# Turning three instead of two of sixteen key blocks on the vector engine in a graph-attention stage

## The reference, cut to what matters

```python
q = (x @ Wq + bq).reshape(n, H, C)      # H, C = 4, 32
attn = jnp.einsum('nhc,mhc->hnm', q, k) / np.float32(np.sqrt(C))
mask = adj == 0.0
neg = jnp.where(mask[None], -jnp.inf, attn)
e = jnp.where(mask[None], 0.0, jnp.exp(neg - jnp.where(all_inf, 0.0, m)))
alpha = e / jnp.where(denom == 0.0, 1.0, denom)
out = jnp.einsum('hnm,mhc->hnc', alpha, v)
```

## Time and profile before

| | |
|---|---|
| median of 3 runs | 1786.12 us (1785.13 to 1786.65) |
| the profiled execution | 1782.96 us, its span 1781.3 us |
| PE busy | 1735.9 us (97%) |
| DVE busy | 1228.6 us (69%) |
| ACT busy | 975.8 us (55%) |
| POOL busy | 895.6 us (50%) |
| mean of DMA | 218 GB/s |

### The profile page before, as it was taken

The page is one execution under the profiler, slowest core; times in us unless marked ns, Lnnn a source line. Parts: engine busy times, 40 slices in busy tenths (PEclk is TensorE's granted clock), DMA queues, the critical chain, the costliest instruction groups (busy, mean ns, idle before and its releaser), DMA issues.

```text
span 1781.3 us, 40266 instructions
## 1 busy us (share of the span) xinstructions
PE 1735.9 (97%) x15000; PEld 1131.3 (64%) x15000; DVE 1228.6 (69%) x2405; ACT 975.8 (55%) x1505; POOL 895.6 (50%) x849
## 2 busy tenths in 40 slices
PE   7999999999998999999999999999999999999996
PEld 3444444444444778877877887778778777644442
DVE  4777775222225889999999999999999999301322
ACT  0110111010103898999999999999999999411101
POOL 0212120112114755778878788788787896540211
PEclk9999999999998999999999999999999999999998
DMA  9866676899996544445445445454454543897981
GB/s 382 325 221 251 254 252 224 278 313 371 332 366 184 186 155 161 155 155 167 150 140 182 150 152 170 156 173 150 142 178 144 167 157 116 323 371 275 321 323 57
DMA packets 134029, 388.53 MB, mean 218 GB/s; under 512 B 15712, under 2 KB 66144, under 8 KB 109280
## 3 DMA queue, kind: packets, MB, share of 16 engines
q1 hardware_dynamic: 117792, 356.11, 57.6%
q10 hardware_dynamic: 13824, 22.75, 3.6%
q0 software_dynamic: 2240, 7.34, 1.6%
HBM read 333.19 MB, written 52.95 MB: 217 GB/s over the span
## 4 chain that ended last, share of the span: by engine, by line
PE 92%; DVE 4%; issue 1%; ACT 1%; DMA 1%; POOL 1%; DVEq 0%; ACTq 0%; POOLq 0%; SPq 0%
PE bank L592 35%; PE bank L742 23%; PE bank L763 14%; PE bank L701 13%; DVE arena L1281 2%; PE bank L580 1%; PE bank L655 1%; PE bank L614 1%; PE bank L613 1%; DMA arena<-x_dram 1%; PE bank L607 0%; PE bank L769 0%; PE bank L650 0%; PE bank L789 0%; PE bank L630 0%
## 5 line engine op out<-in xcount | busy, mean ns | idle before, releaser
L976 ACT ACTIVATE arena<-arena,small 128x2048 f32<-128x2048 f32 x256 | 516.2, 2016 | 2.8 <-DVE small L1281 2.8
L742 PE MATMUL bank<-ident,arena 128*128 128x128 f32 x3592 | 485.5, 278 | 4.4 <-ACT arena L976 2.6
L742 PEld LDWEIGHTS bank<-ident,arena 128*128 128x128 f32 x3592 | 398.1, 141 | 87.8 <-issue 41.9
L592 PE MATMUL bank<-arena,stat_s 128*128 128x512 f32 x1008 | 439.1, 592 | 2.1 <-issue 1.2
L988 ACT ACTIVATE arena<-bank 128x512 f32<-128x512 f32 x673 | 377.0, 604 | 66.2 <-PE bank L742 65.3
L701 PE MATMUL bank<-k,parts 128*128 128x512 f32 x1024 | 354.4, 436 | 10.6 <-DVE small L1281 10.6
L592 PEld LDWEIGHTS bank<-arena,stat_s 128*128 128x128 f32 x1008 | 189.2, 190 | 226.8 <-issue 225.4
L763 PE MATMUL bank<-arena,stat_x 128*32 128x128 f32 x8192 | 276.5, 276 | 0.0
L763 PEld LDWEIGHTS bank<-arena,stat_x 128*32 128x32 f32 x8192 | 208.1, 109 | 90.8 <-issue 81.5
L592 PE MATMUL bank<-arena,stat_x 128*128 128x512 f32 x512 | 228.3, 598 | 10.1 <-DMA arena<-adj_cols 7.8
L701 PEld LDWEIGHTS bank<-k,parts 128*128 128x128 f32 x1024 | 158.8, 192 | 29.6 <-DVE small L1281 24.5
(11 more groups left out here) (155 smaller groups left out, 1431.8 us busy)
## 6 DMA issues: line engine op xcount, KB each, us to landing
arena<-adj_cols SPq DMA_DIRECT2D x190, 1024.0 KB, 6.4
stat_s<-adj SPq DMA_DIRECT2D x85, 512.0 KB, 4.8
group_dram<-stat_s SPq DMA_DIRECT2D x63, 512.0 KB, 2.9
arena<-group_dram SPq DMA_DIRECT2D x252, 128.0 KB, 2.8
arena<-adj SPq DMA_DIRECT2D x43, 512.0 KB, 4.6
parts<-q_dram SPq DMA_DIRECT2D x128, 64.0 KB, 2.4
k<-k_dram POOLq DMA_DIRECT2D x28, 256.0 KB, 9.5
x_dram<-arena ACTq DMA_DIRECT2D x16, 256.0 KB, 3.7
```

What stands on the lines that cost most here:

```text
L592: mm_ = pe.matmul(bank[:, to, :], stat[:, jt, :], ring[:, s, j, :], start=(jt == 0), stop=(jt == TILES - 1))
L742: last = pe.transpose(bank[:, b_, h * P:(h + 1) * P], cols[:, st % SETS, h, u * P:(u + 1) * P], ident[:, :])
L976: act.activation(cols[:, s_, h, :], cols[:, s_, h, :], ACT.Exp, bias=shift[:, t % 2, 1, i:i + 1], scale=-1.0, accum_out=blocksum[:, t % 2, ...
```

## The change: what it does

Units 13, 14 and 15 are turned in blocks, at places 1, 2 and 6, as one group of three. PE turns 13 units a set, 104 a chunk (before 112); in the last set all 16, as before. `slot_of` and `used_before` number the turned slots by PE's units alone. The group gets slots of its own in `stat_s` and `blocks` moves to chunks 5 to 7 of it. One of three mask buffers goes, masks are loaded 7 ahead, and chunks 0 to 5 of `xt` are spilled. The attends run in three batches, at 4, 8 and 14. SP's order becomes: group's store, mask, group's loads, mask, xt's store, queries. The tables of copies and exponents are new: DVE copies 23 of 104 units a chunk (before 28 of 112), ACT 81 (before 84). DVE's `hh` goes from place 113 to 115, ACT's logarithms from 119 to 121. The last product waits for all of `xt` before its first slot, not before its third; `load_xt` also waits for the last group's attends.

```diff
-ATTEND_BATCH = 4
-ATTEND_LAG = 8
-BLOCK_TURN_AT = {14: 3, 15: 5}
-GROUPS = ((14, 15),)
-VECTOR_PLACES = (6,)
-VECTOR_ALSO = (3, 9, 17, 21, 23, 25, 37, 49, 53, 58, 61, 64, 81, 82, 84, 89, 90, 103, 109, 114, 119, 121, 125)
-VECTOR_NOT = (22, 54, 118)
-EXP_MOVED = {1: 3, 5: 7, 13: 12, 21: 22, 29: 28, 37: 39, 45: 44, 49: 51, 53: 54, 57: 58, 61: 60, 69: 70, 73: 74, 77: 76, 81: 83, 85: 84, 89: 87, 93: 90, 101: 103, 105: 106, 109: 108, 113: 114, 121: 122, 125: 124}
+ATTENDS = {4: (-4, -3, -2, -1), 8: (0, 1, 2, 3, 4, 5), 14: (6, 7, 8, 9, 10, 11)}
+BLOCK_TURN_AT = {13: 1, 14: 2, 15: 6}
+GROUPS = ((13, 14, 15),)
+VECTOR_PLACES = ()
+VECTOR_ALSO = (5, 6, 7, 19, 25, 27, 38, 54, 58, 59, 66, 69, 82, 86, 87, 91, 92, 97, 99, 103, 119, 121, 123)
+VECTOR_NOT = ()
+EXP_MOVED = {9: 6, 13: 12, 17: 18, 21: 22, 25: 26, 29: 27, 33: 34, 37: 38, 41: 40, 45: 44, 49: 52, 53: 55, 57: 58, 61: 60, 65: 67, 69: 70, 73: 72, 77: 76, 81: 82, 89: 86, 93: 91, 97: 99, 101: 102, 105: 103, 109: 108, 117: 119, 125: 123}
...
-MASK_AHEAD = 8
-MASKS = 3
-SPILLED = (2, 3, 4, 5)
+MASK_AHEAD = 7
+MASKS = 2
+SPILLED = (0, 1, 2, 3, 4, 5)
...
+def slot_of(k):
+
+    return (PE_UNITS + LAST_UNITS).index(k) % TURNED
+
+
+def used_before(c, k):
+
+    i = (PE_UNITS + LAST_UNITS).index(k) - TURNED
+    return c * UPC + PE_UNITS[i] + 1 if i >= 0 else (c - 1) * UPC + PE_UNITS[i] + 1
...
-        group_slots = arena[:, RING + 10 * CHUNK:RING + 12 * CHUNK]
-        adj_in = (arena[:, RING + 4 * CHUNK:RING + 6 * CHUNK], spilled[:, 0:2 * CHUNK], spilled[:, 2 * CHUNK:4 * CHUNK])
+        adj_in = (arena[:, RING + 4 * CHUNK:RING + 6 * CHUNK], spilled[:, 0:2 * CHUNK])
+        group_slots = spilled[:, 2 * CHUNK:5 * CHUNK]
+        blocks = [stat_s[:, TILES - 3 * TPC:TILES, :].rearrange("p t f -> p (t f)")]
...
-                if g * UPS + GROUPS[i][-1] >= TURNED:
-                    sp.wait_ge(unit_used, g * UPS + GROUPS[i][-1] - TURNED + 1)
+                if g > 0:
+                    sp.wait_ge(unit_used, (g - 1) * UPS + GROUPS[i][-1] + 1)
...
-                    load_mask_ahead(c, 2 * st + 0)
                     if g < GROUP_SETS:
                         store_group(g, 0)
+                    load_mask_ahead(c, 2 * st - 1 if g == 0 else 2 * st)
+                    if g < GROUP_SETS:
+                        load_group(g, 0)
+                    if g == 0:
+                        load_mask_ahead(c, 2 * st)
+                    load_mask_ahead(c, 2 * st + 1)
                     if st == 0 and c - 2 in SPILLED:
                         store_xt(c - 2)
-                    if g < GROUP_SETS:
-                        load_group(g, 0)
                     if st % SETS == 0:
...
-                    load_mask_ahead(c, 2 * st + 1)
...
+                sp.wait_ge(unit_used, GROUP_SETS * UPS)
...
-                    if (k - ATTEND_LAG) % ATTEND_BATCH == 0:
-                        for a in range(k - ATTEND_LAG, k - ATTEND_LAG + ATTEND_BATCH):
-                            if a >= 0:
-                                attend(c, a, first)
-                            elif not first:
-                                attend(c - 1, UPC + a, False)
+                    for a in attended_at(c, k):
+                        if a >= 0:
+                            attend(c, a, first)
+                        elif not first:
+                            attend(c - 1, UPC + a, False)
...
-            product(2, 0, {0: [final_out], SPILLED[0] - 1: [lambda: pe.wait_ge(xt_in_place, 16 * len(SPILLED))], 5: [lambda: pe.wait_ge(att_pool, AG(last - 1, "xt"))],
+            pe.wait_ge(xt_in_place, 16 * len(SPILLED))
+            product(2, 0, {0: [final_out], 5: [lambda: pe.wait_ge(att_pool, AG(last - 1, "xt"))],
```

More of the change, by code:

```diff
@@ L122 @@
 LAST_UNITS = [k for k in range(UPC - UPS, UPC) if k % UPS in BLOCK_TURN_AT]
+LAST_BY_VECTOR, LAST_BY_SCALAR = LAST_UNITS[0::2], LAST_UNITS[1::2]
 def is_block_turned(c, k):
@@ L198, in last_bank_before, with attended_at @@
     return TURN_BANKS.uses[LAST_USE + 1 + LAST_UNITS.index(k) - len(TURN_BANKS.BANKS)][1]
+def attended_at(c, k):
+    u = k % UPS
+    return [k - u + a for a in ATTENDS.get(u, ())]
+def slot_of(k):
[3 more added lines that the diff above has]
+    return c * UPC + PE_UNITS[i] + 1 if i >= 0 else (c - 1) * UPC + PE_UNITS[i] + 1
 BY_VECTOR = [k for k in PE_UNITS if (k % 16 in VECTOR_PLACES or k in VECTOR_ALSO) and k not in VECTOR_NOT]
@@ L287, in build_program @@
         cols = arena[:, 0:RING].rearrange("p (s h n) -> p s h n", s=2, h=H)
+        spilled = stat_s[:, SPILLED[0] * TPC:(SPILLED[-1] + 1) * TPC, :].rearrange("p t f -> p (t f)")
         turned = [stages[i] for i in (0, 1, 6, 7, 2, 3, 10, 11)]
-        group_slots = arena[:, RING + 10 * CHUNK:RING + 12 * CHUNK]
-        spilled = stat_s[:, SPILLED[0] * TPC:(SPILLED[-1] + 1) * TPC, :].rearrange("p t f -> p (t f)")
-        adj_in = (arena[:, RING + 4 * CHUNK:RING + 6 * CHUNK], spilled[:, 0:2 * CHUNK], spilled[:, 2 * CHUNK:4 * CHUNK])
-        tail = stat_s[:, TILES - 2 * TPC:TILES, :].rearrange("p t f -> p (t f)")
-        blocks = [tail if len(group) == 2 else spilled[:, 2 * CHUNK:3 * CHUNK] for group in GROUPS]
+        adj_in = (arena[:, RING + 4 * CHUNK:RING + 6 * CHUNK], spilled[:, 0:2 * CHUNK])
+        group_slots = spilled[:, 2 * CHUNK:5 * CHUNK]
+        blocks = [stat_s[:, TILES - 3 * TPC:TILES, :].rearrange("p t f -> p (t f)")]
         maskbias = [half_[:, i * BLOCK:(i + 1) * BLOCK] for half_ in
@@ L305, in slots_of @@
         def slots_of(i):
-            first, n = GROUPS[i][0] % TURNED - 6, len(GROUPS[i])
-            return group_slots[:, first * CHUNK:(first + n) * CHUNK]
+            return group_slots[:, 0:len(GROUPS[i]) * CHUNK]
         def tiles(ap):
@@ L541, in _ @@
                              q_parts[:, i, :].bitcast(F32)).then_inc(gcn_q_out, 16)
-            load_mask(0, 5)
+            load_mask(0, 4)
             sp.wait_ge(gcn_dve, CV(last, "root"))
             sp.dma_start(root_dram[:, last * CHUNK:CHUNKS * CHUNK], root_out).then_inc(gcn_root_out, 16)
-            for m in range(6, MASK_AHEAD):
+            for m in range(5, MASK_AHEAD - 1):
                 load_mask(0, m)
@@ L761, in attend @@
                     else:
-                        weights = turned[k % TURNED][:, h * P:(h + 1) * P]
+                        weights = turned[slot_of(k)][:, h * P:(h + 1) * P]
                     last = pe.matmul(to, stat_x[:, k % UPT, h * C:(h + 1) * C], weights,
@@ L815, in attention @@
                 if last_chunk:
-                    for a in range(UPC - ATTEND_LAG, UPC):
+                    for a in range(UPC - 4, UPC):
                         attend(c, a, first)
@@ L981, in copy_unit @@
                 if not (first and k < TURNED):
[L982 to L988 removed]
+                    act.wait_ge(unit_used, used_before(c, k))
+                elif k >= TURNED - 2:
+                    act.wait_ge(gcn_x2_out, 16 * CHUNKS)
+                elif k >= TURNED - 4:
+                    act.wait_ge(gcn_k_out, 32 * CHUNKS)
+                act.activation(turned[slot_of(k)], bank[:, unit_bank(k), :],
                                ACT.Copy).then_inc(unit_copied_act, 1)
@@ L1049, in attention @@
                         block_weights(c, k // UPT)
-                    if k in BY_SCALAR or (last_chunk and k == LAST_UNITS[1]):
+                    if k in BY_SCALAR or (last_chunk and k in LAST_BY_SCALAR):
                         copy_unit(c, k, first)
@@ L1377, in attention @@
             def attention(c, first, last_chunk):
-                post = post_steps(c - 1, 107 if last_chunk else 113) if not first else {}
+                post = post_steps(c - 1, 107 if last_chunk else 115) if not first else {}
                 for k in range(UPC):
@@ L1397, in attention @@
                             turn_blocks(c, k - place + u)
-                    if k in BY_VECTOR or (last_chunk and k == LAST_UNITS[0]):
+                    if k in BY_VECTOR or (last_chunk and k in LAST_BY_VECTOR):
                         copy_unit(c, k, first)
```

38 lines of the change are left out of this document (14 added, 24 removed).

## The result

| | before | after |
|---|---|---|
| median of 4 runs | 1785.83 us (1785.13 to 1786.65) | 1815.13 us (1809.0 to 1816.66) |
| the profiled execution | 1782.96 us, span 1781.3 | 1816.66 us, span 1815.0 |
| mean granted clock | 0.993 | 0.984 |

The ratio is 1.0157, with a 95% interval of 1.0134 to 1.0181: 29 us slower. I forecast 1772, with 1755 to 1785 as the range and 0.82 for faster. The forecast was wrong, and the sign too.

The account below looks back on a forecast made before the run. PE was taken as the bound (119.3 of 119.7 us a chunk), with DVE overtaking it after. Seven chunks gain 12.6 us, chunk 0 4.5, the last product loses 3.9: 13.2 off 1786.1, forecast 1772, range 1755 to 1785.

Parts of the forecast that it names:

- PE's need, copies, block transposes: Work per attention chunk: PE falls to 114.3 us, DVE rises to 115.4 and overtakes it, ACT falls to 110.2.
- The first rival: DVE fed without a gap and the chain early enough: a chunk takes 115.4 us, 1754 in all; chance 0.20.
- What four transposes are worth on PE: A turned unit's four PE transposes cost 0.43 us; with 0.25 from joined attend batches, PE gains 0.68 a set.
- The Mobius chain: POOL's chain from mh at place 77 to DVE's reduction, moved to 115: norms 2.0 us late, stretch 36.0 us.
- The xt store comes 6 us later: On SP; POOL's beta_terms waits for it, costing at most 1 us a chunk at DVE's statistics, place 41.
- the other 90 places: A chunk's places outside the Mobius stretch: DVE 80.7 us, PE 80.2, plus 1.2 lost between them.
- The third mask buffer: Two mask buffers instead of three: load and bias take 8.4 us of 14.7, hidden at rate; only phase hurts.
- Chunk 0: First attention chunk, without chain or DVE post steps: PE stays the bound, 4.5 us gained of 5.4.
- The last product: PE waits for all six xt loads before slot 0: 3.9 us lost, bounds 3 to 5.5.
- The group's loads: Landed by 16.7 us of a set, needed at 18.4 (place 4 of the next): hidden with 1.7 us to spare.
- The slower rival: Group lands after PE's attend at place 4, each us beyond costing 63 us; 1798 at 12.5 us; chance 0.08.

Follow-up runs that it names:

- run 8: Changed kernel with xt loads split, DVE's post steps later (statistics at place 46), xt store between group's loads and second mask load: 1774.96 us, ratio 0.9954.
- run 10: As run 8, but without loads of the adjacency's blocks past the first two: 1766.42 us, ratio 0.9906.
- run 4: Changed kernel without loads of the adjacency's blocks past the first two: 1783.72 us, ratio 0.9994.
- run 1: Kernel before, with the xt store moved behind the group's loads and the second mask load on SP: 1805.23 us, ratio 1.0107.
- run 7: Changed kernel with DVE's statistics at place 46 instead of 41, its following post steps and PE's x3 also later: 1786.95 us, ratio 1.0022.
- run 2: Kernel before, with two mask buffers and the changed order of mask loads, xt store right behind the group's store: 1799.51 us, ratio 1.0084.
- run 5: Changed kernel with the final xt loads split: chunks 0, 1, 5 ahead of the ring's loads, the rest waited for after slot 1: 1802.36 us, ratio 1.0098.
- run 3: Changed kernel with the xt store moved from behind the second mask load to behind the group's store: 1814.72 us, ratio 1.0162.
- run 6: Changed kernel with a set's sixteen attends in four batches of four, at places 2, 6, 10, 14: 1848.17 us, ratio 1.0360.
- run 11: As run 8, but with a set's second mask load ahead of the group's loads: 1837.51 us, ratio 1.0306.
- run 12: As run 8, but with a set's first mask load ahead of the group's store: 1788.01 us, ratio 1.0025.

## Why the prediction was wrong, by its own steps

- **PE's need, copies, block transposes: near in size, but DVE does not overtake PE.** In chunks 2 to 6 of run 8 PE is busy 116.0 us (forecast 114.3) and DVE 114.6 (forecast 115.4); without mask loads (run 10) PE's is 115.4. From 119.5 before, PE gained 0.44 us a set, 0.51 without mask loads, where I had 0.68. The work alone takes 116.7 us in chunk 1 (runs 4 and 10), where I had 115.4 as the floor by DVE and 117.9 with the chain. The first rival's 115.4 without a gap wasn't reached even without masks.
- **What four transposes are worth on PE.** Rows 4 gave 0.43 us, which with the batches made 0.68 a set; from 119.4 to 116.7 us a chunk is 0.34 a set, and PE's busy time fell from 1735.9 to 1722.2, 14 us, stretches at the lower clock included. The Trainium skill ("VectorE: DVE Perf Modes", the section on the three transpose paths) has its 390 ns for a 128x128 block in bf16; the 98 us estimated from it for the f32 blocks here are nowhere in the traces.
- **The Mobius chain: borne out**, 35.8 us against 36.0, norms 2.0 us late against 2.
- **The step that failed: "The xt store comes 6 us later, and beta_terms on POOL waits for it: at most 1 us a chunk on DVE's statistics at place 41"**, with 80.7 + 1.2 for the other 90 places, 0.6 of the 1.2 for this. Those took some 88 (123.9 - 35.8), and DVE stood 3.8 us a chunk at place 41 ((23.9 - 1.0 in chunk 1)/6; 4.6 at most). Four things were missed, all on one chain. POOL has no slack from xt to place 41: 31.6 us back to back, y 0.24 us ahead of DVE. xt itself is 2.1 us later against the chunk's first store, as much as the reduction that it comes from is by going from place 113 to 115; I didn't follow what hangs on that move. The store's landing added 1.5 (3.7 in run 1). And shorter places bring DVE to 41 sooner. I read the absence of a wait as room. Run 1 shows the store's place alone at 20 us for four chunks, run 7 gives 28 back by moving the chain's deadline. A chunk from 2 to 6 took 6.0 us more than forecast (123.9 for 117.9): 4.6 of them go in run 7, and run 10, with its store earlier and no mask loads, is at 117.7.
- **The third mask buffer, "at rate it is hidden; only its phase hurts": wrong.** 15 us with the changed order of the mask loads (run 2), 8.5 once the statistics have room (run 10, their traffic included). My working took two masks at even distances; POOL does its biases in pairs between post steps, and a buffer freed by the first is loaded when SP comes to it. It doesn't simply add to the xt term: both make the same chain late.
- **Chunk 0, 4.5 us gained: not so.** By the stores it is even, with 2.9 us gained in sets 1 to 7 (104.5 to 101.6) and 3.0 lost in the first (16.3 to 19.3). But the first store of the kernel before leaves late, at 588.30, behind two mask loads on SP, so the stores are a poor measure there. From DVE's first mask to its 65th it is 119.4 us before and 118.0 after: 1.4 gained. The other runs with the group of three have 116.5 to 119.5 there, so even that isn't sure, and why PE's gain doesn't show is open.
- **The last product, 3.9 us (3 to 5.5): undersized.** 5.8 us, and 1.6 more since the first slot runs at the lower clock; run 5 takes both away.
- **The group's loads, hidden with 1.7 us to spare: held, barely.** PE waits 3.4 us for them in the kernel after (5 times), but runs 3, 6, 11 and 12 show how near it was. The median landings, 4.1 and 3.8 us, are inside my bounds of 4.4 and 4.2, the longest, 6.1 us, is not. The slower rival had the right sign and the wrong place.

In sum the forecast (13.2 us off) and the two spans (33.7 us more) are 46.9 us apart. Of these 29.4 lie in chunks 2 to 6, 7.7 in chunk 7, 4.6 in chunk 0, 1.8 in chunk 1, 1.9 at the start of the last product and 1.5 ahead of and behind all this.

Terms of the same size as the gain (13 us) lay in rows that I hadn't asked for: POOL's timeline over places 0 to 41.

## What to carry to other kernels

A step that shows no wait is not a step with room: look at when its input was ready, and count from there, above all where the change makes everything else faster. When a step is moved by two places, follow its chain into the next stage before calling it free. And where several engines issue in a fixed order, look for a consumer's place to move before undoing the producers: five places on one engine gave back 28 us here, three reorderings of the queue gave nothing or lost.

## What the runs showed of the hardware

- After a gap of 3.42 us on PE inside dense work (ending at 992.06) the granted clock was 0.50, the level of 1.2 GHz, from 992 to 995 and 1.00, the level of 2.4 GHz, from 996 on; a pair of scores took 1.22 us in it instead of 0.71. After the gap of 5.78 us ahead of the product it was 0.50 from 1572 to 1574 and 0.65 from 1574 to 1576, and the first slot took 5.31 us instead of 3.70. So both gaps cost more than their length, the second by 1.6 us.
- 66 MB less traffic in the whole execution (DMA share 0.44 instead of 0.67 in chunk 1) changed PE's and DVE's busy time in that chunk by 1.3 and 0.7 us, about 1%. PE's 1.3 us a chunk are the smaller part of the 31 us that the mask loads cost in the kernel after (run 4); the rest came through waits.
- The group's store landed in 4.1 us (768 KB) where it took 2.9 (512 KB), its loads in 3.8 (192 KB) where they took 2.8 (128 KB). The DMA share in attention rose at the same time, from 0.49 to some 0.65, and the landings of masks, whose size did not change, went from 4.6 and 4.8 to 5.6 and 5.1 us; so size and load aren't separated.
